# Gated cross-attention and routed experts on one core: two norm steps, one residual sum and the rank products stand elsewhere in their engines' queues

## What is computed

```
x = x + tanh(g_xattn) * attention(layernorm(x), ctx)      # 16 heads of 16, 77 keys
x = x + tanh(g_ffn)   * moe(layernorm(x))                 # 8 experts, each token to its top 2
moe: logits = z @ router_w ; probs = softmax ; top_p, top_e = top_k(probs, 2)
     per pair: y = (gelu(z @ w_in[e] + b_in[e]) @ w_out[e] + b_out[e]) * p ; sum per token
```

## Time and profile before

| | us |
|---|---|
| median of 3 runs | 276.29 (276.13 to 279.11) |
| the profiled execution, whole time | 275.26 |
| its span (first to last instruction) | 273.4 |
| PE, DVE, ACT, POOL busy | 237.6, 166.2, 134.9, 143.6 |
| chain that ended last | PE 48%, POOL 14%, DVE 12%, issue 11%, DMA 10%, ACT 3% |

### The profile page before, as it was taken

The page is one execution under the profiler, slowest core; times in us unless marked ns, Lnnn a source line. Parts: engine busy times, 40 slices in busy tenths (PEclk is TensorE's granted clock), DMA queues, the critical chain, the costliest instruction groups (busy, mean ns, idle before and its releaser), DMA issues.

```text
span 273.4 us, 5539 instructions
## 1 busy us (share of the span) xinstructions
PE 237.6 (87%) x1644; PEld 187.0 (68%) x1644; DVE 166.2 (61%) x512; ACT 134.9 (49%) x306; POOL 143.6 (53%) x181
## 2 busy tenths in 40 slices
PE   7899989995699999989688689999999999999900
PEld 4575543653367465734576489999999999999800
DVE  3897957973286548669658026585435343457745
ACT  4347444711771873165314055666566665656520
POOL 3689327327875760003867754444477774446520
PEclk9999999999799999999889979999999999999985
DMA  7910950292233010000222555534353373797365
GB/s 211 340 53 4 448 185 7 78 324 83 77 115 115 17 63 0 2 0 35 82 78 78 154 162 164 161 115 119 118 170 115 106 212 119 223 363 264 116 204 181
DMA packets 25837, 37.34 MB, mean 137 GB/s; under 512 B 3497, under 2 KB 22954, under 8 KB 25714
## 3 DMA queue, kind: packets, MB, share of 16 engines
q1 hardware_dynamic: 21074, 19.91, 24.2%
q0 software_dynamic: 3744, 10.24, 10.4%
q10 hardware_dynamic: 992, 6.84, 7.3%
HBM read 24.64 MB, written 18.39 MB: 157 GB/s over the span
## 4 chain that ended last, share of the span: by engine, by line
PE 48%; POOL 14%; DVE 12%; issue 11%; DMA 10%; ACT 3%; ACTq 0%; POOLq 0%; SPq 0%; DVEq 0%
PE pA L1293 10%; PE pG L1293 9%; PE pM L1293 9%; POOL y_rows L603 8%; DMA stage<-in_w_out 4%; PE pM L1361 4%; PE pA L1622 2%; PE pA L1413 2%; POOL slots L595 2%; PE pA L1399 2%; PE pA L1654 2%; ACT prob L692 2%; PE pA L1419 2%; DVE st L875 2%; POOL rstd L491 2%
## 5 line engine op out<-in xcount | busy, mean ns | idle before, releaser
L603 POOL DMA_INDIRECT y_rows<-y_sb,dst_i x46 | 46.0, 1000 | 40.2 <-ACT y_sb L838 35.9
L1233 DVE TENSOR_TENSOR hT_lo<-pA,hT_hi 128x256 fp32r<-128x256 f32 x46 | 19.5, 424 | 44.3 <-ACT hT_hi L832 44.1
L919 DVE TENSOR_REDUCE mx<-pM 128x4 f32<-128x308 f32 x64 | 27.6, 471 | 21.5 <-PE pM L1361 20.8
L595 POOL DMA_INDIRECT slots<-z2a,pos_u x16 | 16.0, 998 | 29.9 <-DVE pos_u L1133 25.7
L825 ACT ACTIVATE h_sb<-pM 128x256 f32<-128x256 f32 x46 | 17.6, 383 | 23.2 <-PE pM L1293 23.2
L1293 PE MATMUL pM<-win_hi,xT_hi 128*128 x92 | 26.6, 289 | 0.0
L1293 PE MATMUL pM<-win_lo,xT_hi 128*128 x92 | 26.5, 288 | 0.0
L1293 PE MATMUL pM<-win_hi,xT_lo 128*128 x92 | 26.4, 287 | 0.0
L1293 PE MATMUL pA<-wout_hi,hT_lo 128*128 x92 | 25.9, 282 | 0.0
L1293 PE MATMUL pA<-wout_lo,hT_hi 128*128 x92 | 25.9, 281 | 0.0
L1293 PE MATMUL pA<-wout_hi,hT_hi 128*128 x92 | 25.9, 281 | 0.0
(11 more groups left out here) (255 smaller groups left out, 657.1 us busy)
## 6 DMA issues: line engine op xcount, KB each, us to landing
xg<-slots SPq DMA_DIRECT2D x46, 128.5 KB, 2.4
slots<-in_empty ACTq DMA_DIRECT2D x1, 3983.5 KB, 14.8
x_sb<-in_x SPq DMA_DIRECT2D x4, 512.0 KB, 7.1
stage<-in_w_in SPq DMA_DIRECT2D x8, 256.0 KB, 2.7
stage<-in_w_out SPq DMA_DIRECT2D x8, 256.0 KB, 2.6
slots<-in_empty ACTq DMA_DIRECT2D x1, 1927.5 KB, 8.0
yc<-y_rows SPq DMA_DIRECT2D x6, 256.0 KB, 4.5
out<-x_sb SPq DMA_DIRECT2D x6, 256.0 KB, 2.2
```

What stands on the lines that cost most here:

```text
L595: pool.indirect_dma_start(out=slots[GROUP[s]], out_offset=bass.IndirectOffsetOnAxis(ap=pos_u[:, s, q:q + 1], axis=0), in_=z2[int(s > 0)][: ...
L603: pool.indirect_dma_start(out=y_rows[int(j >= JB)], out_offset=bass.IndirectOffsetOnAxis(ap=dst_i[:, j:j + 1], axis=0), in_=y_sb[:, j % YR ...
L919: nc.vector.tensor_reduce(dst[:, 2 * g:2 * g + 2, 2 * h:2 * h + 2], pM[:, g, 0:4 * KV].rearrange("p (r s n) -> p r s n", s=2, n=KV), AX_X, ...
L1233: nc.vector.tensor_tensor(hT_lo[:, j % 2, :], pS[:, 1, 0:D], hT_hi[:, j % 2, :].bitcast(F32), ALU.subtract).then_inc(h_lo, 1)
```

## The change

Six edits, all of place or of idle work:

- POOL: `inv_std(0, 3)` and `inv_std(1, 0)` stand behind two weight units instead of four.
- ACT: block 0's `norm2(0)` stands behind `exp(1, 5)` instead of ahead of `exp(1, 3)`.
- DVE: `residual(2)` stands behind the whole routing of stage 0 instead of ahead of it.
- PE: `ranks(0)` stands behind `scores(3, 0)` instead of behind `scores(3, 1)`. It writes to `pM` instead of `pG`, so it waits until the maxima have been reduced and no longer for `residual(1)` and `residual(2)`.
- PE: the wait until DVE has taken the ranks moves from `project(3, 1)` to `scores(3, 1)`, which is the next to write to `pM`.
- PE: three idle products between `transpose_x(0)` and `transpose_x(1)`, two behind `transpose_x(1)`.

```diff
-        pR = [pG, pS, pG]
+        pR = [pM, pS, pG]
...
-            split_weights(0, 4)
+            split_weights(0, 2)
             inv_std(0, 3, var1, rstd1)
             inv_std(1, 0, var2, rstd2)
-            split_weights(4, 12)
+            split_weights(2, 12)
...
                 split_q(b + 1, 0)
-                if b == 1:
-                    norm2(0)
...
                 exp(b, 4)
                 exp(b, 5)
+                if b == 1:
+                    norm2(0)
...
-            residual(2)
             choose(0, 0)
             choose(0, 1)
             count_first()
             place_pairs(0)
+            residual(2)
             refine(3, 0)
...
                     else:
-                        pe.wait_ge(rank_taken, 1)
                         pe.wait_ge(x1_ready, 3)
...
                 if n == 0:
-                    pe.wait_ge(x1_ready, 3)
+                    pe.wait_ge(sm_red, 16 * BLOCKS)
...
             scores(3, 0)
+            ranks(0)
             scores_rest(3, 0)
             denominators(3, 0)
+            pe.wait_ge(rank_taken, 1)
             scores(3, 1)
-            ranks(0)
...
             transpose_x(0)
+            keep_busy(pA[:, 3, :], w_hi[0], 3)
             transpose_x(1)
+            keep_busy(pA[:, 3, :], w_hi[0], 2)
```

## The result

| | before | after |
|---|---|---|
| median of 4 runs each, us | 277.45 (276.13 to 279.11) | 267.56 (266.37 to 268.23) |
| the profiled execution | 275.26 | 267.75 |
| its span | 273.4 | 265.8 |
| PE, DVE, ACT, POOL busy | 237.6, 166.2, 134.9, 143.6 | 236.9, 166.9, 134.3, 143.2 |

The ratio of the times is 0.9636 [0.9561, 0.971]. The forecast was 269.2 and faster; the measured median is 1.6 us under it. The two profiled executions differ by 275.26 - 267.75 = 7.5 us, against a sum of 7.1. The medians differ by 9.9, and the interval of this ratio, 8 to 12 us, doesn't hold 7.5. What the traces can explain is the 7.5 us between the two profiled executions; no trace shows the other 2.4 us of this pair.

A forecast was written before the change was run, and what follows sets the result against it. PE was taken as the bound (48% of the chain), held in block 1 by ACT, POOL and a DMA, later pacing the experts. 5.9 + 0.2 + 1.0 = 7.1 us less: 276.29 - 7.1 = 269.2; range 266.7 to 272.1.

The forecast's parts named there:

- Term 1: Block 1: norm moved behind the exponentials removes PE's stall and the low clock behind it; 5.9 us, bounds 4.65 and 6.2.
- the sum without it: Whole kernel: gain if activity did not keep PE's clock up, 4.65 + 0.2 - 0.5 = 4.35 us.
- The rival of a new wait behind the norm: Block 1: ACT's norm, copy and inverse delay DVE up to the projection; gain there only 4.65 us, time 270.4, chance 0.10.
- the two halves are not to be added: Block 1: POOL's half of the edit alone would give nearly the same gain as both, and adds little to ACT's.
- Unit 4 starts at about 66.6: POOL's weight units: transfer issued at 64.0 lands 2.6 us later, so later units run 1 us early; 1.6 us slack.
- the slower rival: POOL's units 4 to 11: late transfers cost 5.5 us each, from two on the kernel is slower, 278.6; chance 0.03.
- The routing: Last block: routing ahead of residual(2) readies places 3.7 us early, but little follows; 0.2 us, bounds 0 and 0.3.
- The new wait of POOL: Last block: POOL stands about 3.5 us for nm behind three sends, at block 2's inverse deviation.
- The rival of the earlier places getting through: Last block: all sends go on 3.7 us earlier, time 265.5; against it, the inverse deviation in POOL's queue; chance 0.05.
- The idle products: Start of the experts: five idle products keep PE's clock up; 1.0 us less, bounds 1.5 less and 0.5 more.
- the 1.6 us at the fast end: From 135.2 to 139.0, untouched by the change: half the stretch at clock 0.55 may fall otherwise; 1.6 us in the range.
- The other signs of being wrong: norm2(1) waiting for nb, or the first expert tile over 1 us sooner behind the variance of block 3.

The follow-up runs named there:

- act_only: The kernel before with only ACT's edit, block 0's second norm moved behind exp(1, 5): 277.64 us against 284.96 for before on the same chip, ratio 0.9735.
- pool_only: The kernel before with only POOL's edit, two inverse deviations behind two weight units instead of four: 278.72 us against 284.96 for before on the same chip, ratio 0.9819.
- inv11_behind_14: The kernel after with inv_std(1, 1) behind fourteen weight units instead of twelve on POOL: 272.41 us, 3.3 us more than the unchanged kernel after on that chip.
- inv_behind_six: The kernel after with block 2's and block 3's inverse deviations three sends later on POOL: 265.46 us against 269.08 for the unchanged kernel after on that chip.
- after_again: The kernel after, unchanged, measured again on another occasion: 269.08 us against 275.95 for before there, ratio 0.9731.
- before_fill: The kernel before with 18 idle products in block 1's stall, ahead of scores_rest(1, 1): 282.0 us against 283.71 for before on that chip, ratio 0.9944.
- after_no_idle: The kernel after without the five idle products at the start of the experts: 279.06 us against 284.96 for before on that chip, ratio 0.978.
- before_idle5: The kernel before with only the five idle products at the start of the experts: 283.5 us against 283.71 for before on that chip, ratio 0.996.

## Why the prediction was right

**Block 1, the wait and its price.** Right in each step. `scores_rest(1, 1)` was forecast at 66.15 and stands at 66.09; the next piece was to take 2.40 us and took 2.49; the norm was to start at 68.2 without a wait and starts at 67.89; the projection was forecast at 77.2 and stands at 77.33. Term 1 was 5.9, and from `scores(1, 1)` to `scores(2, 0)` the stages show 5.78 - 0.05 = 5.73. The clock's share is needed for this: the sum without it, 4.35 us, is far below the 7.5 between the profiled executions. The rival of a new wait behind the norm fell with it, and "the two halves are not to be added" was shown by act_only and pool_only.

**The POOL side.** "Unit 4 starts at about 66.6" was wrong: it starts at 68.13, since its transfer, issued at 64.09, took 4.0 us until the split could start and not 2.6. The units gained nothing, POOL delivered `nb` at 87.7 instead of 86.7, and ACT asked at 88.43. The slack was 0.7 us and not 1.6. It held, but the kernel after stands closer to the slower rival than the prediction said, and inv11_behind_14 shows what lies behind it.

**The routing.** Right: 0.2 forecast, 0.28 measured in stretch B, and 0.18 up to the first tile (5.91 against 5.73 in the table of stages). The new wait of POOL was forecast at about 3.5 us and is 3.67. The rival of the earlier places getting through did not happen, for the reason given against it; inv_behind_six confirms the reason by removing it. It also shows that this rival was priced too high: of 3.7 us only about 1.9 would have got through at an unchanged clock, since PE's idle products ahead of the first tile are next.

**The idle products.** Right in size where they work: 5.91 to 6.92 in the table of stages is 1.0 us. "They push the first expert product by 0 to 0.5" was 0.05. That the profiled execution of after was one of the seven in which they worked is luck: with the 8.26 us of after_again the term would have been 0.2. Working in one execution and not in another was priced by the range, not by the term. So was block 3's projection, the 1.6 us at the fast end for a place that the change doesn't touch: before_fill showed it, at 1.5 us.

**The forecast and the medians.** The 1.6 us between the forecast and the median are mostly not the mechanism's. The sum was 0.4 us short (7.1 against 7.5). The other 1.2 lie in how the profiled execution stands to the median, which the forecast took over from before: it lay 1.0 us below before's three runs, and 0.2 us above after's four.

**The end.** The stages sum to 7.03 at the last scatter. The 0.6 us that remain in the span lie behind it: from there to the end it is 11.8 us instead of 12.4, in the last transfers, which the change doesn't touch. The pace of 2.11 us didn't change. The other signs of being wrong stayed away as well: `norm2(1)` did not wait for `nb`, and the first tile stands 13.6 us behind block 3's inverse deviation, where it had stood 13.5.

## What to carry to other kernels

Read what stands behind a waiting instruction in its own queue: a wait that nobody needs yet costs whatever is queued behind it, through as many engines as hand it on, and the first link that is cheap to cut is enough. A twin of the stage without the stall gives the price of removing it, clock included. And an earlier result gains nothing while its consumer's queue holds a later wait: when you bring a producer forward, look at the consumer's queue in the same edit, and then at what the next engine does meanwhile: here moving one small step on POOL by three sends, and dropping eight idle products that had become the bound, was worth 3.7 us by the stages. (The medians differ by 6.1; the rest went with a clock that stood better in those executions.)

## What was not expected of the hardware

**Chips differ.** The kernel before takes 277.45 and 275.95 us on chips 1 and 3, and 284.96 and 283.71 on chips 2 and 4. Each chip was used on one occasion, so chip and occasion can't be told apart. Up to the experts the traces agree within some 1.2 us on a stretch (A of the kernels with the stall is 23.54 on chip 1, 24.77 on chip 4). The excess is in the expert phase: from the first `transpose_x` to the last product of PE it is 104.1 us in before and 103.0 in after on chip 1, 103.7 in after_again on chip 3, and 112.7 in act_only, 113.3 in after_no_idle (chip 2) and 111.7 in before_idle5 (chip 4). It comes in a few long gaps between two tiles, and they lie at the same place of the program in all eight traces of chips 2 and 4, whatever the kernel. Count the steps from one `transpose_h` to the next. Past the very first tiles, the first step over 3 us is always the one behind tile 18 (counted from 0), and the last is behind tile 22 to 26. From tile 15 to tile 37 these traces lie 7.9 to 10.4 us above the pace of 2.11 us per tile, and the six others 0.5 to 0.7 us. Here two rows of act_only, on ACT and on PE:

```profile
211.07 0.38 ACT L825 ACTIVATE h_sb<-pM 128x256 f32<-128x256 f32 x1 [3.92 <-remote]
```

```profile
212.34 0.41 PE L1654 MATMUL pA<-cst,h_sb 128*128 128x128 f32 x2 [3.17 <-DVE hT_lo L1233]
```

The trace names "remote" and "issue" as what ended many of ACT's and DVE's waits there; the cause stays open.

**The clock is not fixed by the program.** The same products at the start of the experts ran 7.43 us in one execution of the kernel after and 8.26 in another, and over the kernels block 3's projection took 4.90 to 4.97 us in nine executions and 3.45 in three, behind the same ten idle products. A term of about 1 us that rests on the clock should carry the other level in its range.
